# Retention on one Trainium2 core: the split keys are turned by a transposing transfer on the SyncE queue, not by TensorE

## What is computed

```
gammas = 1.0 - 2.0 ** (-5.0 - jnp.arange(h, dtype=jnp.float32))
q = (x @ W_q.T).reshape(b, t, h, dh)
k = (x @ W_k.T).reshape(b, t, h, dh)
v = (x @ W_v.T).reshape(b, t, h, dh)
decay = jnp.where(diff >= 0, gammas[:, None, None] ** pow_, 0.0)
attn = jnp.einsum('bihd,bjhd->bhij', q, k) * decay[None] / scale
y = jnp.einsum('bhij,bjhd->bihd', attn, v)
```

## Time and profile before

| | us |
|---|---|
| median of three runs (lowest, highest) | 1824.58 (1823.99, 1827.91) |
| the profiled execution's own time | 1825.66 |
| its span in the trace | 1823.7 |
| PE busy over the span | 1380.7 (76%) |
| DVE busy | 1373.2 (75%) |
| ACT busy | 1255.7 (69%) |
| POOL busy | 1222.6 (67%) |

### The profile page before, as it was taken

How to read it: one execution, slowest core, us unless ns; L and a number is a source line. 1 busy time by engine, 2 the same in 40 slices (tenths; PEclk the granted TensorE clock), 3 DMA queues, 4 the chain that set the end, 5 groups by cost and what they waited for, 6 DMA issues and landing times. The chain is left out here.

```text
span 1823.7 us, 63408 instructions
## 1 busy us (share of the span) xinstructions
PE 1380.7 (76%) x21895; PEld 953.2 (52%) x21896; DVE 1373.2 (75%) x3576; ACT 1255.7 (69%) x3382; POOL 1222.6 (67%) x1312
## 2 busy tenths in 40 slices
PE   3559999968899455455517888888886799999857
PEld 3425555545555244444414666666664566666646
DVE  7877777766566489889838989898974688888748
ACT  7728888846666478788847777777743577777745
POOL 6748777733333588767426888888864677777747
PEclk9999999989999877777758999999999999999959
DMA  8636777779998557666534655555543122222228
GB/s 259 213 104 185 194 196 191 195 157 209 207 221 218 182 148 197 184 161 168 150 86 99 114 119 113 119 113 119 105 91 78 38 52 52 52 52 52 52 85 292
DMA packets 495360, 256.33 MB, mean 141 GB/s; under 512 B 359357, under 2 KB 484864, under 8 KB 494720
## 3 DMA queue, kind: packets, MB, share of 16 engines
q1 hardware_dynamic: 482658, 219.11, 49.7%
q0 software_dynamic: 12576, 35.67, 6.3%
HBM read 79.52 MB, written 73.44 MB: 84 GB/s over the span
## 5 line engine op out<-in xcount | busy, mean ns | idle before, releaser
L213 PE MATMUL ps<-all_late,l_xq_T 128*128 128x352 f16 x1536 | 245.0, 317 | 40.7 <-DMA l_xq_T<-l_apart 30.9
L213 PE MATMUL ps<-l0moe_W,all_xT_all 128*128 128x16 f16 (+2 forms) x1152 | 190.8, 312 | 39.3 <-ACT all_xT_all L911 22.3
L213 PEld LDWEIGHTS ps<-all_late,l_xq_T 128*128 (+1 forms) x1536 | 151.6, 99 | 120.4 <-DMA l_xq_T<-l_apart 31.3
L1443 POOL TENSOR_TENSOR all_late<-experts_se,all_mhalf 128x4 f32<-128x4 f32 (+1 forms) x77 | 76.4, 992 | 159.6 <-DVE experts_se L1552 153.6
L618 PE MATMUL ps<-all_late,ffn_hT 128*128 128x256 f16 x1088 | 130.0, 273 | 58.3 <-ACT l_xq_T L682 57.2
L2296 POOL TENSOR_TENSOR all_late<-ret_pm,all_late 128x512 f16<-128x512 f32 x128 | 145.5, 1158 | 19.3 <-ACT all_late L2202 19.3
L618 PEld LDWEIGHTS ps<-all_late,ffn_hT 128*128 128x128 f16 x1088 | 101.6, 98 | 91.3 <-ACT l_xq_T L682 64.6
L213 PEld LDWEIGHTS ps<-l0moe_W,all_xT_all 128*128 128x128 f16 x1152 | 84.1, 100 | 121.5 <-ACT all_xT_all L911 26.0
L364 POOL TENSOR_TENSOR ffn_h<-ffn_fq_val,ffn_h 128x704 f16<-128x704 f32 x64 | 97.3, 1521 | 50.0 <-ACT ffn_h L359 50.0
L213 PE MATMUL ps<-moe_E,experts_gT 128*128 x864 | 117.6, 276 | 15.8 <-DMA experts_gT<-slots_dram 11.0
L1708 PE MATMUL ps<-l_kvm,both_q 128*128 128x136 f16 x384 | 38.3, 268 | 119.8 <-DVE both_o L1881 119.8
(11 more groups left out here) (299 smaller groups left out, 4717.0 us busy)
## 6 DMA issues: line engine op xcount, KB each, us to landing
rows_dram<-all_late SPq DMA_DIRECT2D x72, 256.0 KB, 2.9
ret_v<-ret_vpad SPq DMA_DIRECT2D x256, 64.0 KB
front_xin<-x SPq DMA_DIRECT2D x16, 512.0 KB, 4.3
x_dram<-front_x SPq DMA_DIRECT2D x16, 512.0 KB, 5.1
all_late<-x_dram SPq DMA_DIRECT2D x64, 128.0 KB
z_dram<-all_late SPq DMA_DIRECT2D x64, 128.0 KB
both_zin<-z_dram SPq DMA_DIRECT2D x16, 512.0 KB, 4.7
both_xin<-x SPq DMA_DIRECT2D x16, 512.0 KB, 4.1
```

The costliest lines, as they stand in the source:

```text
L213: mm = pe.matmul(out, lhs[a], rhs[b], start=first and n == 0, stop=last and n == 2, skip_group_check=True)
L1443: pool.tensor_tensor(rows[:, n % 4, which, :, 0], se[:, u, which], power[:, which], ALU.pow).then_inc(s_time, 1)
```

## The change

`kd16` is turned by a transposing transfer. SyncE gets a stage `turn` for tile c-2, behind `spread`: it waits for both halves of `kd16` and for the slot to be free, and issues one transfer of 128 x 512 float16 into `kT`, a ring of three tiles in SBUF (two new ones and a part of `late`), with one semaphore per slot. TensorE's `turn` is gone, as is `turned` in PSUM; its waits on the halves of `kd16` stand in `updates` now. `results` no longer waits for `keys_T` of the tile two on. `keys_T` reads SBUF instead of PSUM.

```diff
--- before.py
+++ after.py
@@ -2005,22 +2005,23 @@
         scores_w, keys_w = U * 2 * 4 * RC, U * 2 * C * P * 2
         p16 = late[:, 0:scores_w].rearrange("p (u a r k) -> p u a r k", u=U, a=2, r=4)
         kx16 = late[:, scores_w:scores_w + keys_w].rearrange("p (u a c s e j) -> p u a c s e j", u=U, a=2, c=C, s=SUBS, e=2)
+        kT = [ph.sb(f"kT{n}", [P, 2 * C, P], F16)[:] for n in range(U - 1)]
+        kT.append(late[:, scores_w + keys_w:scores_w + keys_w + 2 * C * P].rearrange("p (k m) -> p k m", m=P))
         qd = ph.sb("qd", [P, U, C, P])
         q16 = ph.sb("q16", [P, U, 2, C, P], F16)
         pm = ph.sb("pm", [P, U, 4, RC])
         told = ph.sb("told", [P, U, SUBS, CW])
         state = ph.sb("state", [P, U, SUBS, CW])
         st16 = ph.sb("st16", [P, U, 2, SUBS, CW], F16)
-        (s_fill, s_zero, s_kv, s_q, s_vhi, s_vlo, s_kd, s_qd, s_kdhi, s_kdlo, s_qhi, s_qlo, s_turn, s_kx, s_u, s_t0, s_r1,
+        (s_fill, s_zero, s_kv, s_q, s_vhi, s_vlo, s_kd, s_qd, s_kdhi, s_kdlo, s_qhi, s_qlo, s_kx, s_u, s_t0, s_r1,
          s_t1, s_r0, s_sthi, s_stlo, s_s, s_p, s_phi, s_plo, s_y, s_yev, s_stat, s_pass, s_spass) = ph.sems(
-            "fill zero kv q vhi vlo kd qd kdhi kdlo qhi qlo turn kx u t0 r1 t1 r0 sthi stlo s p phi plo y yev stat pass spass")
-        s_vx = [ph.sem(f"vx{n}") for n in range(U)]
+            "fill zero kv q vhi vlo kd qd kdhi kdlo qhi qlo kx u t0 r1 t1 r0 sthi stlo s p phi plo y yev stat pass spass")
+        s_vx, s_turn = ([ph.sem(f"{n}{u}") for u in range(U)] for n in ("vx", "turn"))
         sps = ps[:, 0:4, 0:RC]
         ups = ps[:, 0:SUBS, RC:RC + CW]
         qps = ps[:, 2, RC:2 * RC].rearrange("p (c m) -> p c m", c=C)
         kt, vps = ([ps[:, 4 + u, at:at + D] for u in range(U)] for at in (0, D))
         yps = ps[:, 7, 0:D].rearrange("p (c m) -> p c m", c=C)
-        turned = ps[:, 7, D:2 * D].bitcast(F16)
         block = ph.enter_context(nc.Block())
         passes = ((0, 0), (1, 0), (0, 1))
 
@@ -2046,11 +2047,21 @@
                         src = vpad[s * SUB:(s + 1) * SUB, t.slot4, e * 2 * D:(e + 1) * 2 * D]
                         dst = v16[e * SUB:(e + 1) * SUB, t.slot4, s].rearrange("p k d -> p (k d)")
                         sp.dma_start(dst, src).then_inc(s_vx[t.slot4], 16)
-            pipeline(sp, TILES, [(3, spread)], 3)
+
+            def turn(t):
+                sp.wait_ge(s_kx, ago(t, 3))
+                through(sp, s_spass)
+                sp.wait_ge(s_kdhi, after(t))
+                through(sp, s_spass)
+                sp.wait_ge(s_kdlo, after(t))
+                through(sp, s_spass)
+                sp.dma_start_transpose(kT[t.slot4], kd16[:, t.slot4].rearrange("p k d -> p (k d)")
+                                       ).then_inc(s_turn[t.slot4], 16)
+            pipeline(sp, TILES, [(3, spread), (2, turn)], 3)
 
         @block.tensor
         def _(pe):
-            prime_wrap(pe, s_kv, s_q, s_turn, s_u, s_s, s_y)
+            prime_wrap(pe, s_kv, s_q, s_u, s_s, s_y)
 
             def scores(t):
                 pe.wait_ge(s_kx, after(t))
@@ -2073,18 +2084,9 @@
                                                 skip_group_check=True)
                 ins.then_inc(s_s, 1)
 
-            def turn(t):
+            def updates(t):
                 pe.wait_ge(s_kdhi, after(t))
                 pe.wait_ge(s_kdlo, after(t))
-                pe.wait_ge(s_kx, ago(t, 1))
-                pe.wait_ge(s_yev, ago(t, 3))
-                for part in range(2):
-                    for c in range(C):
-                        at = (part * C + c) * P
-                        ins = pe.transpose(turned[:, at:at + P], kd16[:, t.slot4, part, c * P:(c + 1) * P], ident[:])
-                ins.then_inc(s_turn, 1)
-
-            def updates(t):
                 pe.wait_ge(s_vhi, after(t))
                 pe.wait_ge(s_vlo, after(t))
                 pe.wait_ge(s_p, ago(t, 1))
@@ -2109,8 +2111,6 @@
                 pe.wait_ge(s_plo, after(t))
                 pe.wait_ge(s_vx[t.slot4], 64 * (t.n // U) + 64)
                 pe.wait_ge(s_yev, ago(t, 1))
-                if not isinstance(t.n, int) or t.n + 2 < TILES:
-                    pe.wait_ge(s_kx, ago(t, -2))
                 for c in range(C):
                     for s in range(SUBS):
                         for n, (a, b) in enumerate(passes):
@@ -2153,7 +2153,7 @@
                             ins = pe.matmul(qps[:, j], w[a], x[:, b * C + c], start=c == 0 and n == 0 and j == 0,
                                             stop=c == C - 1 and n == 2, skip_group_check=True)
                 ins.then_inc(s_q, 1)
-            pipeline(pe, TILES, [(4, scores), (3, turn), (0, project), (3, updates), (2, queries), (5, results)], 3, head=0)
+            pipeline(pe, TILES, [(4, scores), (0, project), (3, updates), (2, queries), (5, results)], 3, head=0)
 
         @block.scalar
         def _(act):
@@ -2177,9 +2177,9 @@
                 ins.then_inc(s_vhi, 1)
 
             def keys_T(t):
-                act.wait_ge(s_turn, after(t))
+                act.wait_ge(s_turn[t.slot4], 16 * (t.n // U) + 16)
                 act.wait_ge(s_s, ago(t, 3))
-                src = turned.rearrange("p (k j) -> p k j", j=SUB)
+                src = kT[t.slot4].rearrange("p k (s j) -> p (k s) j", j=SUB)
                 for e in range(2):
                     ins = act.activation(kx16[:, t.slot4].rearrange("p a c s e j -> p (a c s) e j")[:, :, e], src,
                                          ACT.Copy, scale=parity[:, e:e + 1])
@@ -2188,7 +2188,8 @@
             def keys_hi(t):
                 act.wait_ge(s_kd, after(t))
                 act.wait_ge(s_u, ago(t, 3))
-                act.wait_ge(s_turn, ago(t, 3))
+                if not isinstance(t.n, int) or t.n >= U:
+                    act.wait_ge(s_turn[t.slot4], 16 * (t.n // U))
                 act.activation(kd16[:, t.slot4, 0], kd[:, t.slot4], ACT.Copy).then_inc(s_kdhi, 1)
 
             def queries_hi(t):
```

## The result

| | before | after |
|---|---|---|
| median of the runs (lowest, highest), us | 1824.53 (1823.79, 1827.91) | 1837.05 (1833.33, 1838.23) |
| ratio, 95% interval | | 1.0062 [1.0049, 1.0075] |
| span of the profiled execution, us | 1823.7 | 1831.5 |
| PE, DVE, ACT, POOL busy, us | 1380.7, 1373.2, 1255.7, 1222.6 | 1366.0, 1384.2, 1257.2, 1221.8 |

The change makes the kernel 0.6% slower, 12.5 us by the medians and 7.8 by the two spans. The forecast was 1821.6, and the time lies above its range. TensorE has 14.7 us less to do, as step (a) counted (15.4), and VectorE has 11 us more, though the change has no line of VectorE's in it.

A forecast was written before the change was run, and what follows sets the result against it. TensorE was taken as the pace, held in one cycle of three by VectorE and that by GpSimd. 2.9 us over 19 passes plus 0.1 outside gave 3 less, 1821.6 us; range 1809 to 1836, the forecast's own 1818.5 to 1824.

The forecast's parts named there:

- (a): TensorE's queue: loses four transposes, 0.24 us a tile, 15.4 us for 64 tiles at most.
- (f): Waits dropped from `results` and moved to `updates`, for values ready a cycle earlier: 0 both ways.
- (b): TensorE's `updates` waits for `masked` plus 0.21 us: at most 0.27 us a pass comes through.
- rival B: GpSimd's `scores_lo` gets ahead of VectorE's `states` (L2256) in the first cycle: 8 us more, 1833; chance 0.10.
- (c): Chain behind: next `masked` follows VectorE's list, 6.35 us from `keep_result`; moves only by the second cycle's 0.12.
- the idle 1.02: VectorE, first cycle: `masked` starts 1.02 us behind the end of `statistics`, read as VectorE's own loop branch.
- (d): ScalarE's `keys_T` reads SBUF instead of PSUM: 0.04 to 0.08 us more for the pair.
- (e): SyncE's transposing transfer: 1.2 us of queue, lands in 2.8, hidden with 0.6 us to spare, cost 0.
- A: Transfer lands late and paces the chain from 4.1 us on: 13 to 33 us more, 1838; chance 0.16.
- C: TensorE's gain comes through, `masked` shifting with `scores`: 12 us less, 1812.6; chance 0.18.
- the forecast's 0.15: Gain per pass of the loop, taken as the middle between 0.04 and 0.27 us.

The follow-up runs named there:

- the control: Kernel before, `turn` still on TensorE, with the wait of `updates` on `masked` put behind its other waits: 1823.85 us, ratio 0.9985.
- the moved waits: Changed kernel, `scores_lo` held for L2257, waits for both halves of `kd16` put ahead of `project` instead of in `updates`: 1821.72 us, ratio 0.9986.
- `masked` last: Changed kernel, `scores_lo` held for L2257, the wait of `updates` on `masked` put behind its five others: 1817.71 us, ratio 0.9960.
- queries first: Changed kernel, `scores_lo` held for L2257, `queries` moved to free PSUM bank 7, ahead of `updates` (TensorE) and `states` (VectorE): 1812.71 us, ratio 0.9938.
- the hold alone: Changed kernel with one wait more: GpSimd's `scores_lo` waits for VectorE's L2257 of the tile one on: 1827.34 us, ratio 1.0019.

## Why the prediction was wrong, step by step

**What failed, in short.** The sum had 3 us less; the kernel came out 12.5 us slower. Two things had been put at nothing in it. Step (f) gave the two moved waits "0 both ways": they cost 0.26 us a pass, and with them step (b)'s 0.21 us from `masked` to `updates` became 0.36. And the tie of rival B, left out of the sum with a chance of 0.10, went the wrong way: 0.40 us a pass.

**The account.** Per pass of the loop, from the traces: 15.26 before; 0.27 less in the control, nearly all of it a shorter idle time at the branch (14.99); 0.28 less without `turn` (14.71, `masked` waited for last); 0.30 more with the two moved waits ahead of `project`, which starts 0.11 later by them, and two waits behind `masked` (15.01); 0.26 more with five behind `masked` (15.27); 0.40 more for the collision. That is 15.67, as measured. The first four nearly cancel, so the loss of the pass is the collision's size.

The account is of passes, not of the whole time. The control's pass says 5.1 us less than before, its ratio 2.7 (1.1 to 4.4); the moved waits, `masked` last and queries first also lie 2 to 5 us higher against the kernel before than 19 of their passes say, and so does the hold alone (3.5 us, with an equal pass). One execution of each kernel was traced, so whether the kernel before has its 0.96 us at the branch in all of them is not known. The variants' differences among each other agree better with their passes (7.8 against 7.6 us for the collision, 6.0 against 4.9 for the moved waits).

**(a), TensorE's queue: right.** 14.7 us less busy against 15.4.

**(b), how much comes through: the premise failed, and the size agrees by luck.** The 0.21 us from `masked` to `updates` was read off the kernel before and taken for a constant. It is made of the waits that stand behind: in the changed kernel it is 0.36, and `updates` stays at 2.21 us behind `scores`. The step had 0.12 in the second cycle, 0.15 in the third and 0 in the first. With 0.21 restored (moved waits ahead of `project`), `updates` does start at 2.06 to 2.10, as forecast, but nothing of it reaches the pass: the next `scores` does not come earlier in the second cycle (4.83, as before); the second half of `results` took 0.61 to 0.64 instead of 0.55 there. Why is not settled. With `masked` waited for last the sum is 0.28, next to the step's 0.27, but with 0.15 in place of 0.21 and cycle by cycle otherwise: 0.19 and 0.23 less in the second and third, 0.14 more in the first.

**(f), waits dropped and moved: the step that failed first.** "0 both ways" was argued from the values being ready. Ready they were; but the build put five waits behind `masked` instead of two, and the queue's walk over them cost 0.15 us where TensorE was already late, 0.26 a pass, 5 us.

**(c), the chain behind: failed as a reading.** `masked` follows `scores`, not VectorE's list; the idle 1.02 was not VectorE's branch alone, since it is 0.75 in the changed kernel and 1.56 with `masked` last. The other half was right: `next_state` is held by GpSimd and ends 1.24 behind its start.

**(d), (e): right.** L2184 went from a mean of 695 ns to 724, 0.03 more for each. The transfer is hidden: ScalarE waited 3.2 us for it in all, and 64 unused transfers in the kernel before cost 1.0006 [0.9997, 1.0016].

**The rivals.** A fell with (e). C did not come: with `turn` gone, the collision held off and `masked` last, the pass is 0.28 under the control, 5.3 us and not C's 12. The kernel with queries first is faster by more, but it is another program. B happened: `scores_lo` at 1562.80, L2257 at 1562.87, end 1.24 behind GpSimd's start. Its sum was 0.6 a pass less the forecast's 0.15, 0.45; the pass lost 0.41. That the two are so near is luck: B alone was 0.40, not 0.6, and the gain of 0.15 did not come. It got 0.10 because its condition was a tie that could not be read to 0.1 us. But the tie was pushed from both sides. In the first cycle of the kernel before, L2256 starts 3.24 us behind `scores` and `scores_lo` 3.55: a lead of 0.31. The change moves `scores_lo` to 3.34, since `keys_T` no longer waits, and, by the moved waits, L2257 to 3.43. Either shift alone is less than the lead, the two together are more. By these numbers B would not have come without the error of (f); that was not run. The rule of the Trainium skill ("SBUF — State Buffer", section "SBUF: two separate sides"), that in such a pair the second of the two engines is blocked for all of the other's instruction, agrees with these runs: 0.23 alone, 1.17 when 0.07 late. The other rule quoted ("VectorE: DVE Perf Modes", section "The three transpose paths") would have made the transfer the loss; without transfers the pass was as long, 15.70 against 15.67.

## What to carry to other kernels

When an edit frees one engine, list which pairs of instructions on the other engines now change places, and which of them share something (here VectorE and GpSimd, both on SBUF): a tie there is a risk of a whole instruction's length, and a wait that holds back the longer one can be worth more than the freedom. A wait on a value long since ready cost least here when it stood ahead of the wait that binds; see in the built program where it stands, and put the binding wait last. And a latency read off one kernel is a sum of things that the edit may change.

## What the runs showed of the hardware

- Met waits behind the one that binds cost TensorE time: 0.36 us from the end of `masked` to `updates` with five, 0.21 with two, 0.15 with none. That is 0.03 to 0.05 us each, if it goes by the wait.
- TensorE's idle time at the branch of a hardware loop of some 600 matmuls differs from build to build: 0.96 (kernel before), 0.82, 0.70, 0.66, in one kernel 0.70 and 0.85 in turns. In the traces that alone makes up to 0.3 us a pass, 0.3% of this kernel for 19 passes; the control, which has 0.26 of it, was 0.15% faster (0.06 to 0.24). The cause is open.
- A VectorE operation of 128 x 64 float32 with both inputs in SBUF takes 0.23 us alone and 1.17 when it starts 0.07 us behind a GpSimd operation of some 1.15 us on SBUF.
- A transposing transfer of 128 x 512 float16 costs 1.19 us of SyncE's queue, and 64 of them nothing in time beside four plain ones a tile.
